# Self-attention by pairs and quads of heads, with f16 parts for Q, K, V, transposes by DMA, and a reordered last chunk before it

## The chip, the cores and the metric

The kernel runs on one core of a Trainium2 chip. The metric is the device time of one execution, in microseconds (us); less is better.

## The reference, cut to what matters

```python
# x: 1 x 256 x 512, ctx: 1 x 25088 x 512
# first attention: the 256 x 512 queries are read as 128 tokens of 16 heads of 64,
# the context as 12544 keys of 16 heads of 64
x = x + attention(layernorm(x) @ wq.T + bq, ctx @ wk.T + bk, ctx @ wv.T + bv)
# second attention
h = layernorm(x)
k, v, q = split(h @ w_in.T)                    # 512 -> 3 * 512
logits = q k^T / sqrt(32) + bias[h, i - j]     # 16 heads of 32, 256 x 256 per head
x = x + softmax(logits) @ v
x = x + mixture_of_experts(layernorm(x))       # 8 experts, top 2, hidden 1024
```

The bias is a sum of 16 Gaussians of the distance i - j, for each head.

## The kernel before

Three stages follow each other on one core; the order on each engine is the order in which the code is written, and semaphores join the engines.

**Cross-attention.** The context comes in 49 chunks of 512 rows (`NCH`), one `step(c)` each. PE projects K and V of chunk c+1 while chunk c is scored in four groups of four heads (`scores`), weighted (`weigh`) and added (`add_o`). Softmax goes through `maxima` and `p_lows` on DVE, `exps` and `p_highs` on ACT, and the running sums are rescaled on POOL. Each probability is split into two f16 parts (high on ACT, low on DVE), and both parts of a group are transposed by DMA, issued by SP (`turn_p`). f32 values are multiplied as three f16 products (`THREE`): high by high, low by high, high by low. The projected blocks share four PSUM banks (`ps_proj`), the scores have the two of `ps_s`, the output the two of `ps_o`. In the last chunk (c = 48, `NCH - 1`) no projection is left, and the scores of a group wait until the exponentials of the group before have been read from `ps_s`. SP loads all of `w_in` (3 MB) in step 47.

**Self-attention.** The residual is formed (L948), normalised, transposed on PE in f32 (`turn`), and multiplied with the f32 `w_in` (L1252, L1259). The bias rows go to DRAM and come back as diagonals (L312, L316). Then a loop over 16 heads runs one head at a time: `scores` of head h (L1272), the transposes of head h-1 on PE (L1283), the product with V of head h-3 (L1293). DVE forms logits and maxima (L987, L991), ACT the exponentials (L664), and ACT and DVE split the transposed probabilities (L657, L977).

**Experts.** 32 pieces of weights are loaded by SP (`load_piece`), split by ACT (L645) and DVE (L965), and multiplied by PE (L1316, L1339), from 1364.63 us to the end.

## Time and profile before

| | us |
|---|---|
| median of 3 runs (lowest, highest) | 1622.64 (1620.98, 1627.67) |
| the profiled execution, its own time | 1625.82 |
| its span, first to last instruction | 1624.1 |
| PE busy | 1556.1 |
| DVE busy | 1318.7 |
| ACT busy | 1260.3 |
| POOL busy | 923.4 |

The rows below are of this one execution. PE is the matrix engine, DVE the vector engine, ACT the scalar engine, POOL GpSimd; SPq is the queue of SyncE, which issues DMAs. In a timeline row the first number is the start, the second the duration in us, and in square brackets stands how long the engine sat idle before it and who released it. Times are counted from the first instruction.

### The profile page before, as it was taken

The numbers are of one execution on the slowest core, as the hardware profiler recorded it, in microseconds if no ns is written. First come the engines' busy times: TensorE is split into PE (matmuls) and PEld (weight loads), VectorE is DVE, ScalarE is ACT, GpSimd is POOL, SyncE is SP. The second block draws the span as 40 slices with busy tenths as digits, with TensorE's granted clock in tenths as the row PEclk, the third lists the DMA queues.
The fourth block names the chain that finished last, engine by engine and source line by source line (L and its number), as shares of the span: only waits on it lengthen the run. The fifth ranks groups of instructions, "written<-read, shape, count | busy, mean of one in ns | idle before, by whom it ended". The sixth has DMA issues, their size and how long they took to land.

```text
span 1624.1 us, 47795 instructions
## 1 busy us (share of the span) xinstructions
PE 1556.1 (96%) x17748; PEld 1279.1 (79%) x17748; DVE 1318.7 (81%) x1764; ACT 1260.3 (78%) x3074; POOL 923.4 (57%) x938
## 2 busy tenths in 40 slices
PE   7999999999999999999999999999997787999998
PEld 5787888888888888888888888888775555777776
DVE  7788888888888888888888888888986466767675
ACT  4888888888888888988988888888886254655554
POOL 5667678777787787787787787787752000000000
PEclk9999999999999999999999999999998766999999
DMA  4365555555555555645545545545546720555550
GB/s 175 86 135 101 136 137 115 136 131 120 136 123 123 135 119 128 140 111 134 142 107 138 138 108 136 137 115 136 129 81 157 210 103 22 201 206 194 199 206 36
DMA packets 442690, 216.03 MB, mean 133 GB/s; under 512 B 416768, under 2 KB 422912, under 8 KB 436112
## 3 DMA queue, kind: packets, MB, share of 16 engines
q1 hardware_dynamic: 442352, 215.07, 51.6%
q8 instruction: 34, 0.56, 0.1%
q10 hardware_dynamic: 288, 0.27, 0.1%
q14 instruction: 16, 0.13, 0.0%
HBM read 111.96 MB, written 0.56 MB: 69 GB/s over the span
## 4 chain that ended last, share of the span: by engine, by line
PE 85%; DVE 6%; DMA 3%; issue 2%; ACT 1%; POOL 1%; SPq 1%; DVEq 0%; POOLq 0%; ACTq 0%
PE ps_proj L1147 50%; PE ps_proj L1316 10%; PE ps_s L1193 8%; PE ps_o L1211 8%; PE ps_o L1339 5%; DMA pt_s<-p_s 2%; PE ps_proj L1176 1%; PE ps_s L1272 1%; DVE p_s L852 1%; DVE cmax L839 1%; DVE wsp L965 1%; PE ps_proj L1283 1%; POOL ctx_s L380 1%; DMA wst<-w_dram 1%; SPq L316 1%
## 5 line engine op out<-in xcount | busy, mean ns | idle before, releaser
L1147 PE MATMUL ps_proj<-wv_s,ctx_s 128*128 128x256 f16 x4032 | 482.9, 274 | 2.5 <-ACT ps_proj L529 2.5
L1147 PE MATMUL ps_proj<-ctx_s,wk_s 128*128 128x256 f16 x4032 | 480.5, 273 | 4.0 <-ACT ps_proj L527 3.1
L1147 PEld LDWEIGHTS ps_proj<-wv_s,ctx_s 128*128 128x128 f16 x4032 | 381.0, 98 | 65.4 <-issue 11.8
L1147 PEld LDWEIGHTS ps_proj<-ctx_s,wk_s 128*128 128x128 f16 x4032 | 380.0, 98 | 66.5 <-issue 24.7
L380 POOL TENSOR_TENSOR ctx_s<-t_f,ctx_s 128x512 f16<-128x512 f32 x192 | 264.0, 1384 | 279.7 <-ACT ctx_s L475 279.7
L573 ACT ACTIVATE prob<-ps_s,nmax 128x256 f32<-128x256 f32 x784 | 360.1, 475 | 14.8 <-DVE nmax L846 14.5
L839 DVE TENSOR_REDUCE cmax<-ps_s 128x4 f32<-128x1024 f32 x196 | 239.8, 1223 | 130.5 <-PE ps_s L1193 130.3
L852 DVE SCALAR_TENSOR_TENSOR p_s<-prob,p_s 128x1024 f16<-128x1024 f32 x196 | 322.0, 1643 | 2.0 <-ACT p_s L584 2.0
L380 POOL TENSOR_TENSOR ctx_s<-ctx_f,ctx_s 128x512 f16<-128x512 f32 x144 | 214.8, 1492 | 15.4 <-ACT ctx_s L470 10.7
L584 ACT ACTIVATE p_s<-prob 128x1024 f16<-128x1024 f32 x196 | 206.7, 1055 | 6.7
L1211 PE MATMUL ps_o<-v_s,pt_s 128*128 128x64 f16 x4704 | 172.2, 194 | 12.7 <-DMA pt_s<-p_s 12.7
L1316 PE MATMUL ps_proj<-x_s,wsp 128*128 128x256 f16 x1536 | 180.3, 275 | 4.2 <-issue 3.2
L1211 PEld LDWEIGHTS ps_o<-v_s,pt_s 128*128 128x128 f16 x4704 | 165.7, 99 | 22.4 <-DMA pt_s<-p_s 16.2
L1316 PEld LDWEIGHTS ps_proj<-x_s,wsp 128*128 128x128 f16 x1536 | 151.2, 99 | 36.4 <-issue 3.5
L1193 PE MATMUL ps_s<-k_s,q_s 64*128 64x256 f16 x2352 | 164.3, 273 | 6.7 <-ACT prob L573 6.6
L573 ACT ACTIVATION_READ_ACCUMULATOR prob<-ps_s,nmax 128x1 f32 x784 | 162.8, 208 | 0.0
L965 DVE SCALAR_TENSOR_TENSOR wsp<-wst,wsp 128x1024 f16<-128x1024 f32 x96 | 114.5, 1221 | 47.7 <-ACT wsp L645 47.7
L1193 PEld LDWEIGHTS ps_s<-k_s,q_s 64*128 64x128 f16 x2352 | 99.3, 94 | 58.1 <-issue 39.1
L861 DVE TENSOR_TENSOR v_s<-ps_proj,v_s 128x512 f16<-128x512 f32 x192 | 127.4, 685 | 19.2 <-ACT v_s L549 15.9
L549 ACT ACTIVATE v_s<-ps_proj 128x512 f16<-128x512 f32 x192 | 108.8, 600 | 26.1 <-PE ps_proj L1147 26.1
L645 ACT ACTIVATE wsp<-wst 128x1024 f16<-128x1024 f32 x96 | 97.4, 1049 | 19.3 <-DMA wst<-w_dram 19.2
L366 POOL TENSOR_TENSOR t_f<-ctx_f,t_f 128x512 f32<-128x512 f32 x48 | 102.7, 2140 | 0.0
(163 smaller groups left out, 1815.7 us busy)
## 6 DMA issues: line engine op xcount, KB each, us to landing
ctx_f<-ctxt_dram SPq DMA_DIRECT2D x48, 1024.0 KB, 5.8
wst<-w_dram SPq DMA_DIRECT2D x96, 512.0 KB, 4.8
pt_s<-p_s SPq DMA_TRANSPOSE x392, 2.7
w_in_sb<-w_in_dram SPq DMA_DIRECT2D x1, 3072.0 KB, 11.6
tisa<-tisa_scores SPq DMA_DIRECT2D x3, 1024.0 KB, 12.1
w_f<-wk_dram SPq DMA_DIRECT2D x2, 512.0 KB, 5.4
ctx_f<-ctxt_dram SPq DMA_DIRECT2D x2, 512.0 KB, 6.8
w_f<-wv_dram SPq DMA_DIRECT2D x1, 1024.0 KB, 9.7
```

The source lines that it names most:

```text
L380: pool.tensor_tensor(out=low[:, n, :, :], in0=sources[n], in1=high[:, n, :, :], op=ALU.subtract).then_inc(ctx_low, 1)
L549: ins = act.activation(out_v(0, odd, i, j), ps, ACT.Copy)
L573: ins = act.activation(prob[:, g % 2, (2 * b + r) * HC:(2 * b + r + 1) * HC], ps_s[:, b, r * HC:(r + 1) * HC], ACT.Exp, bias=nmax[odd][:, ...
L584: act.activation(p_s[:, g % 2, 0, :], prob[:, g % 2, :], ACT.Copy, scale=P_SCALE).then_inc(p_high, 1)
L839: dve.tensor_reduce(cmax[:, g % 2, :], ps_s[:, :, :].rearrange("p b (r k) -> p (b r) k", r=2), AX, ALU.max).then_inc(cmax_done, 1)
L852: dve.scalar_tensor_tensor(out=p_s[:, g % 2, 1, :], in0=prob[:, g % 2, :], scalar=P_SCALE, in1=p_s[:, g % 2, 0, :], op0=ALU.mult, op1=ALU. ...
L861: ins = dve.tensor_tensor(out_v(1, odd, i, j), ps, out_v(0, odd, i, j), ALU.subtract)
L965: dve.scalar_tensor_tensor(out=wsp[1][:, i % 2, n, :], in0=wst[:, i, n, :], scalar=FW_SCALE, in1=wsp[0][:, i % 2, n, :], op0=ALU.mult, op1 ...
L1147: ins = pe.matmul(ps_proj[:, bank(h, role), sub * QUARTER:(sub + 1) * QUARTER], lhsT, rhs, start=(fresh and sub == 0 and t == 0 and i == 0 ...
L1193: ins = pe.matmul(ps_s[:, head, r * HC:(r + 1) * HC], q_s[a][rows, g, r * P:(r + 1) * P], k_s[odd][b][rows, g, r * HC:(r + 1) * HC], start ...
L1211: ins = pe.matmul(ps_o[:, vg // 2, col:col + DK], pt_s[:, vg, a, 4 * head + tile, :], v_s[vodd][b][:, tile, u * DK:(u + 1) * DK], start=(i ...
L1316: ins = pe.matmul(ps_proj[:, u % 2, m * T:(m + 1) * T], wsp[a][:, (u // 2) % 2, m, col:col + P], x_s[b][:, t, :], start=(t == 0 and k == 0 ...
```

## The change

**Before self-attention.** `w_in` comes in three loads of 1 MB: K in step 46, Q and V in step 47. ACT and DVE split each into f16 parts, one instruction each for every half (`w_in_highs`, `w_in_lows`): K in step 47, Q and V after the last chunk. In the last chunk the scores of groups 1 and 3 go to `ps_proj` (`score_bank`), so two groups can be open; PE and DVE have an order of their own (`last_step`). The residual of each half is divided and added before the last product (`last_base`), which then enters in `last_o`. The bias rows leave for DRAM during the last chunk. `o_acc`, `nmax` and `lsum` are laid out by halves in all chunks, with the same instructions.

**Self-attention.** ACT and DVE split the transposed input directly from PSUM (`x_highs`, `x_lows`). Q and K of four heads come from one PSUM bank (`project_kq`: 24 products of 256 columns; `project_v2`: 12 of 512), and are split by `kq_highs`, `kq_lows`, `v2_highs` and `v2_lows`, one instruction each. Scores are made for four heads at once (`scores2`), and logits, exponentials and splits go by pairs of heads. The factor 4096 of the probabilities is a shift of the exponent, by one more small instruction. The low part is made by POOL, and the two parts are transposed by DMA (`turn_p2`) and not by PE; the pieces 1 to 3 of the experts' weights are loaded behind these transposes. The output is normalised by halves (`attended`). Lines marked "..." are left out.

```diff
-                        sp.wait_ge(ctx_low, UNITS * NCH)
-                        sp.dma_start(w_in_sb[:, :, :], w_in).then_inc(w_in_loaded, 16)
+                    for i, at, used in ((K, (NCH - 3, 0), LAST), (Q, (NCH - 2, 0), NCH), (V, (NCH - 2, 2), NCH)):
+                        if isinstance(c, int) and (c, g) == at:
+                            sp.wait_ge(ctx_low, UNITS * used)
+                            sp.dma_start(w_in_f[i][:, :, :], w_in_dram[i]).then_inc(w_in_loaded[i], 16)
+                    if isinstance(c, int) and (c, g) == (LAST, 1):
+                        sp.wait_ge(tisa_out, 1)
+                        sp.dma_start(tisa_dram.ap().rearrange("h o m -> h (o m)"),
+                                     reli[0:H2, :].bitcast(F32)).then_inc(tisa_stored, 16)
             cross_steps(sp, step)
...
+            def turn_p2(p):
+                if p >= 2:
+                    sp.wait_ge(pv2_done, 2 * (p - 1))
+                for k, split in enumerate((p2_high, p2_low)):
+                    sp.wait_ge(split, p + 1)
+                    sp.dma_start_transpose(pt2_s[:, p % 2, k, :, :], p2_s[:, p % 2, k, :]).then_inc(turned2[p % 2], 16)
+            for p in range(PAIRS):
+                turn_p2(p)
             for i in range(1, 4):
                 load_piece(i, i)
...
             cross_steps(pool, step)
+            for p in range(PAIRS):
+                half = slice(2 * (p % 2), 2 * (p % 2) + 2)
+                pool.wait_ge(p2_high, p + 1)
+                pool.tensor_tensor(out=p2_s[:, p % 2, 1, :], in0=prob2[:, half, :].rearrange("p h c -> p (h c)"),
+                                   in1=p2_s[:, p % 2, 0, :], op=ALU.subtract).then_inc(p2_low, 1)
...
+            def w_in_highs(i, half):
+                act.wait_ge(w_in_loaded[i], 16)
+                act.activation(w_in_s[i][0][:, 2 * half:2 * half + 2, :], w_in_f[i][:, 2 * half:2 * half + 2, :], ACT.Copy,
+                               scale=FW_SCALE).then_inc(w_in_high[i], 1)
...
+                    if isinstance(c, int) and c == NCH - 2:
+                        if h == 0:
+                            act.wait_ge(unit_done, units_through(2 * LAST))
+                        w_in_highs(K, h)
...
+            act.wait_ge(unit_done, units_through(2 * NCH))
+            for i in (Q, V):
+                for half in range(2):
+                    w_in_highs(i, half)
...
+            def exps2(p):
+                act.wait_ge(nmax2_done, p + 1)
+                if p >= 2:
+                    act.wait_ge(p2_low, p - 1)
+                for j in range(2):
+                    for r in range(2):
+                        slot, h = 2 * (p % 2) + j, 2 * p + j
+                        ins = act.activation(prob2[:, slot, r * T:(r + 1) * T], logit[:, slot, r * T:(r + 1) * T], ACT.Exp,
+                                             bias=nmax2[:, p % 2, 2 * j + r:2 * j + r + 1], accum_out=lsum2[:, h // 8, r, h % 8:h % 8 + 1])
+                ins.then_inc(exp2_done, 1)
+            def p2_highs(p):
+                act.wait_ge(exp2_done, p + 1)
+                if p >= 2:
+                    act.wait_ge(turned2[p % 2], 32 * (p // 2))
+                act.activation(p2_s[:, p % 2, 0, :], prob2[:, 2 * (p % 2):2 * (p % 2) + 2, :].rearrange("p h c -> p (h c)"),
+                               ACT.Copy).then_inc(p2_high, 1)
...
+            kq_highs(0)
+            kq_highs(1)
+            for p in range(PAIRS):
+                exps2(p)
+                if p < 2:
+                    kq_highs(2 + p)
+                p2_highs(p)
+                if p == 1:
+                    v2_highs(0)
+                    v2_highs(1)
...
+            def last_base(half):
+                cols = slice(NB * half, NB * half + NB)
+                dve.wait_ge(scaled, 2 * LAST + half + 1)
+                dve.wait_ge(added, 2 * LAST - 1 + half)
+                link(dve.reciprocal(l_acc[:, cols], l_acc[:, cols]))
+                acc3 = o_acc[:, half, :, :, :].rearrange("p r u d -> p (r u) d")
+                link(dve.tensor_tensor(acc3, acc3, l_acc[:, cols].unsqueeze(2).to_broadcast([P, NB, DK]), ALU.mult))
+                link(dve.scalar_tensor_tensor(out=by_rows(stream, half), in0=o_acc[:, half, :, :, :]
+                                         .rearrange("p r u d -> p r (u d)"), scalar=1.0 / (P_SCALE * W_SCALE),
+                                         in1=by_rows(xb, half), op0=ALU.mult, op1=ALU.add))
...
+            def last_o(half):
...
+                dve.wait_ge(pv_done, NG * LAST + 2 * half + 2)
+                acc3 = o_acc[:, half, :, :, :].rearrange("p r u d -> p (r u) d")
+                dve.tensor_tensor(acc3, ps_o[:, half, :].rearrange("p (u d) -> p u d", u=NB),
+                                  l_acc[:, cols].unsqueeze(2).to_broadcast([P, NB, DK]), ALU.mult).then_inc(added, 1)
+                dve.wait_ge(added, 2 * LAST + half + 1)
+                link(dve.scalar_tensor_tensor(out=by_rows(stream, half), in0=o_acc[:, half, :, :, :]
+                                              .rearrange("p r u d -> p r (u d)"), scalar=1.0 / (P_SCALE * W_SCALE),
+                                              in1=by_rows(stream, half), op0=ALU.mult, op1=ALU.add))
+                return stats(stream, half)
...
+            def last_step():
+                block_lows(LAST, 1, C21, LAST % 2)
+                maxima(LAST, 0, LAST % 2)
+                p_lows(LAST - 1, 3)
+                maxima(LAST, 1, LAST % 2)
+                add_o(LAST - 1, 0)
+                tisa_scores()
+                p_lows(LAST, 0)
+                add_o(LAST - 1, 1)
+                maxima(LAST, 2, LAST % 2)
+                p_lows(LAST, 1)
+                maxima(LAST, 3, LAST % 2)
+                last_base(0)
+                p_lows(LAST, 2)
+                p_lows(LAST, 3)
+                last_o(0)
+                last_base(1)
+                link(last_o(1))
+            cross_steps(dve, lambda c, odd: step(c, odd) if not isinstance(c, int) or c < LAST else last_step() if c == LAST else None)
...
+            w_in_lows(Q, 0)
+            w_in_lows(Q, 1)
...
+            def x_lows(i):
+                for r in range(2):
+                    dve.wait_ge(x_high, 2 * i + r - 1)
+                    dve.tensor_tensor(x_s[1][:, :, r * P:(r + 1) * P], ps_s[:, r, :].rearrange("p (t c) -> p t c", t=DT),
+                                      x_s[0][:, :, r * P:(r + 1) * P], ALU.subtract).then_inc(x_split, 1)
...
+            def logits(p):
+                if p % 2 == 0:
+                    dve.wait_ge(tisa_loaded[p // 2], 48)
+                    dve.wait_ge(s2_done, p // 2 + 1)
+                if p >= 2:
+                    dve.wait_ge(exp2_done, p - 1)
+                slots = slice(2 * (p % 2), 2 * (p % 2) + 2)
+                for j in range(2):
+                    h, slot = 2 * p + j, 2 * (p % 2) + j
+                    bias = bass.AP(tisa, h * 3 * P + 2 * P - 1, [[H2 * 3 * P, P], [P, 2], [-1, 2 * P]])
+                    ins = dve.scalar_tensor_tensor(out=logit[:, slot, :].rearrange("p (r k) -> p r k", r=2),
+                                                   in0=ps_proj[:, slot, :].rearrange("p (r k) -> p r k", r=2),
+                                                   scalar=float(HD) ** -0.5 / A_SCALE ** 2, in1=bias, op0=ALU.mult, op1=ALU.add)
+                ins.then_inc(logit_done, 1)
+                dve.wait_ge(logit_done, p + 1)
+                dve.tensor_reduce(nmax2[:, p % 2, :], logit[:, slots, :].rearrange("p h (r k) -> p (h r) k", r=2), AX, ALU.max,
+                                  negate=True).then_inc(max2_done, 1)
+                dve.wait_ge(max2_done, p + 1)
+                dve.tensor_scalar(nmax2[:, p % 2, :], nmax2[:, p % 2, :], P_SHIFT, None, ALU.add).then_inc(nmax2_done, 1)
...
+            def attended(half):
...
+                dve.wait_ge(exp2_done, 4 * half + 4)
+                link(dve.reciprocal(lsum2[:, half, :, :], lsum2[:, half, :, :]))
+                dve.wait_ge(pv2_done, 8 * half + 8)
+                link(dve.tensor_tensor(o_acc[:, half, :, :, :].rearrange("p r u d -> p (r u d)").rearrange("p (g d) -> p g d", d=HD),
+                                       ps_s[:, half, :].rearrange("p (g d) -> p g d", d=HD),
+                                       lsum2[:, half, :, :].rearrange("p r h -> p (r h)").unsqueeze(2)
+                                       .to_broadcast([P, 2 * 8, HD]), ALU.mult))
+                link(dve.scalar_tensor_tensor(out=stream[:, :, cols], in0=o_acc[:, half, :, :, :].rearrange("p r u d -> p r (u d)"),
+                                              scalar=1.0 / A_SCALE, in1=stream[:, :, cols], op0=ALU.mult, op1=ALU.add))
+                return stats(stream, half)
...
+            def last_step():
+                odd = LAST % 2
+                scores(LAST, 0, odd)
+                scores(LAST, 1, odd)
+                tisa_scores()
+                weigh(LAST - 1, 2, 1 - odd)
+                weigh(LAST - 1, 3, 1 - odd)
+                scores(LAST, 2, odd)
+                scores(LAST, 3, odd)
+                for g in range(NG):
+                    weigh(LAST, g, odd)
+            cross_steps(pe, lambda c, odd: step(c, odd) if not isinstance(c, int) or c < LAST else last_step() if c == LAST else None)
...
+            def project_kq(e):
+                if e == 0:
+                    pe.wait_ge(w_in_low[K], 2)
+                    pe.wait_ge(w_in_low[Q], 2)
+                for n, i in enumerate((K, Q)):
                     for t in range(DT):
-                        ins = pe.matmul(ps_proj[:, b + e // 2, (e % 2) * T:(e % 2 + 1) * T],
-                                        w_in_sb[:, t, base + e * P:base + (e + 1) * P], xnT[:, t, :], start=(t == 0),
-                                        stop=(t == DT - 1))
-                ins.then_inc(qkv_done, 1)
...
+            def scores2(e):
+                pe.wait_ge(kq_low, e + 1)
+                if e:
+                    pe.wait_ge(logit_done, 2 * e)
+                for r in range(2):
+                    for n, (a, b) in enumerate(THREE):
+                        for j in range(4):
+                            rows = slice(HD * j, HD * j + HD)
+                            ins = pe.matmul(ps_proj[:, j, r * T:(r + 1) * T], kq_s[a][rows, e, 1, r * P:(r + 1) * P],
+                                            kq_s[b][rows, e, 0, :], start=(n == 0), stop=(n == 2))
+                ins.then_inc(s2_done, 1)
+            def weigh2(p):
+                pe.wait_ge(turned2[p % 2], 32 * (p // 2) + 32)
...
+            project_kq(0)
+            project_kq(1)
+            scores2(0)
+            project_kq(2)
+            project_kq(3)
+            project_v2(0)
+            project_v2(1)
+            scores2(1)
+            weigh2(0)
+            scores2(2)
+            weigh2(1)
+            weigh2(2)
+            scores2(3)
+            for p in range(3, PAIRS):
+                weigh2(p)
             turn(2)
```

On PE, in the last chunk, the instructions stood in this order (`ps_s<-k_s,q_s` are the scores of a group, `ps_o<-v_s,pt_s` the weighting, the row with `tisa_e` the bias rows):

```order
L1193 MATMUL ps_s<-k_s,q_s 128x256 x12
L1211 MATMUL ps_o<-v_s,pt_s 128x64 x24
L1193 MATMUL ps_s<-k_s,q_s 128x256 x12
L1211 MATMUL ps_o<-v_s,pt_s 128x64 x24
L1108 MATMUL ps_s<-tisa_e,tsel 16x512 x2
L1211 MATMUL ps_o<-v_s,pt_s 128x64 x48
L1097 MATMUL ps_s<-ident,xn 128x128 x8
```

and now stand, from the scores of group 0 on:

```order
L1351 MATMUL ps_s<-k_s,q_s 128x256 x12
L1351 MATMUL ps_proj<-k_s,q_s 128x256 x12
L1262 MATMUL ps_proj<-tisa_e,tsel 16x512 x2
L1369 MATMUL ps_o<-v_s,pt_s 128x64 x48
L1351 MATMUL ps_s<-k_s,q_s 128x256 x12
L1351 MATMUL ps_proj<-k_s,q_s 128x256 x12
L1369 MATMUL ps_o<-v_s,pt_s 128x64 x96
L1252 MATMUL ps_s<-ident,xn 128x128 x8
```

Two groups are scored before anything is weighted, and the bias rows come third, with the weighting of the chunk before behind them. On PE, from the projections into the head loop, before:

```order
L1252 MATMUL ps_proj<-xnT,w_in_sb 128x256 x32
L1259 MATMUL ps_o<-w_in_sb,xnT 128x512 x4
L1272 MATMUL ps_s<-kT_s,qT_s 128x256 x6
L1259 MATMUL ps_o<-w_in_sb,xnT 128x512 x4
L1272 MATMUL ps_s<-kT_s,qT_s 128x256 x6
L1283 MATMUL ps_proj<-ident,prob 128x128 x4
L1272 MATMUL ps_s<-kT_s,qT_s 128x256 x6
L1283 MATMUL ps_proj<-ident,prob 128x128 x4
L1272 MATMUL ps_s<-kT_s,qT_s 128x256 x6
L1283 MATMUL ps_proj<-ident,prob 128x128 x4
L1293 MATMUL ps_proj<-v_s,pT_s 128x32 x12
L1272 MATMUL ps_s<-kT_s,qT_s 128x256 x6
```

and now, up to the last weighting (`kq_s` rows are the scores of four heads, `ps_s<-v_s,pt_s` the weighting):

```order
L1426 MATMUL ps_o<-x_s,w_in_s 128x256 x48
L1449 MATMUL ps_proj<-kq_s 128x256 x24
L1426 MATMUL ps_s<-x_s,w_in_s 128x256 x48
L1436 MATMUL ps_o<-w_in_s,x_s 128x512 x24
L1449 MATMUL ps_proj<-kq_s 128x256 x24
L1465 MATMUL ps_s<-v_s,pt_s 128x32 x24
L1449 MATMUL ps_proj<-kq_s 128x256 x24
L1465 MATMUL ps_s<-v_s,pt_s 128x32 x48
L1449 MATMUL ps_proj<-kq_s 128x256 x24
L1465 MATMUL ps_s<-v_s,pt_s 128x32 x120
```

The transposes of the probabilities are gone from PE, and there are four groups of scores in place of sixteen. On SP, from the last load of the context on, before:

```order
L272 DMA ctx_f<-ctxt_dram 128x2048
L293 DMA_TRANSPOSE pt_s<-p_s 128x8x128 x16
L307 DMA w_in_sb<-w_in_dram 128x6144
L293 DMA_TRANSPOSE pt_s<-p_s 128x8x128 x14
L312 DMA tisa_scores<-reli 16x512
L316 DMA tisa<-tisa_scores 128x16x128 x3
L323 DMA wst<-w_dram 128x1024 x3
L326 DMA wg_sb<-wg_dram 128x32
L323 DMA wst<-w_dram 128x1024 x9
```

and now, from the first load of `w_in` on (both kinds of transposes carry the name `pt_s` here; 16 of them are of self-attention):

```order
L330 DMA w_in_f<-w_in_dram 128x2048
L316 DMA_TRANSPOSE pt_s<-p_s 128x8x128 x8
L330 DMA w_in_f<-w_in_dram 128x2048
L316 DMA_TRANSPOSE pt_s<-p_s 128x8x128 x4
L330 DMA w_in_f<-w_in_dram 128x2048
L316 DMA_TRANSPOSE pt_s<-p_s 128x8x128 x6
L333 DMA tisa_scores<-reli 16x512
L316 DMA_TRANSPOSE pt_s<-p_s 128x8x128 x4
L342 DMA tisa<-tisa_scores 128x4x128 x12
L349 DMA wst<-w_dram 128x1024 x3
L352 DMA wg_sb<-wg_dram 128x32
L360 DMA_TRANSPOSE pt_s<-p_s 128x8x128 x16
L349 DMA wst<-w_dram 128x1024 x9
```

The one load of 3 MB became three with transposes between them; the bias rows moved ahead of the last four transposes of cross-attention.

## Rows read from the trace of the kernel before

**Rows 1.** The page, parts 1 and 4: busy engines, and the chain by engine

```profile
PE 1556.1 (96%) x17748; PEld 1279.1 (79%) x17748; DVE 1318.7 (81%) x1764; ACT 1260.3 (78%) x3074; POOL 923.4 (57%) x938
...
PE 85%; DVE 6%; DMA 3%; issue 2%; ACT 1%; POOL 1%; SPq 1%; DVEq 0%; POOLq 0%; ACTq 0%
```

**Rows 2.** Windows: span, busy PE PEld DVE ACT POOL (instructions), clock, DMA share, GB/s

```profile
1280.70:1303.30 22.60, 19.15 (x73) 14.79 (x74) 5.86 (x6) 6.17 (x7) 0.00 (x0) 0.93 0.96 335
1303.30:1354.10 50.80, 46.38 (x360) 31.72 (x360) 33.24 (x51) 27.35 (x82) 0.00 (x0) 0.58 0.13 50
...
1364.60:1400.00 35.40, 34.36 (x275) 26.25 (x276) 22.63 (x56) 19.84 (x31) 0.00 (x0) 0.93 0.37 134
1400.00:1621.00 221.00, 219.58 (x1672) 163.30 (x1669) 152.72 (x210) 121.32 (x193) 0.00 (x0) 1.00 0.48 171
```

**Rows 3.** Timeline, end of step 47 and last chunk (start, duration, what)

```profile
1229.04 0.57 SPq L307 DMA_DIRECT2D w_in_sb<-w_in_dram  x1
...
1233.67 1.48 PE L1147 MATMUL ps_proj<-wv_s,ctx_s 128*128 128x256 f16 x12
...
1242.62 1.13 PE L1211 MATMUL ps_o<-v_s,pt_s 128*128 128x64 f16 x24 [3.99 <-DMA pt_s<-p_s]
...
1243.57 2.75 PE L1147 MATMUL ps_proj<-wv_s,ctx_s 128*128 128x256 f16 x12
...
1246.25 0.92 PE L1193 MATMUL ps_s<-k_s,q_s 64*128 64x256 f16 x12
...
1251.31 1.46 PE L1193 MATMUL ps_s<-k_s,q_s 64*128 64x256 f16 x12 [3.34 <-ACT prob L573]
```

**Rows 4.** Timeline, from the last `p_lows` to the projections

```profile
1267.22 1.22 DVE L852 SCALAR_TENSOR_TENSOR p_s<-prob,p_s 128x1024 f16<-128x1024 f32 x1 [1.95 <-ACT p_s L584]
...
1271.40 0.87 PE L1211 MATMUL ps_o<-v_s,pt_s 128*128 128x64 f16 x24 [0.52 <-DMA pt_s<-p_s]
...
1277.93 1.97 PE L1097 MATMUL ps_s<-ident,xn 128*128 128x128 f32 x8 [5.65 <-DVE xn L725]
...
1280.68 15.71 PE L1252 MATMUL ps_proj<-xnT,w_in_sb 128*128 128x256 f32 x64 [0.78 <-DVE xnT L732]
```

**Rows 5.** Timeline, one period of the head loop

```profile
1341.33 1.46 PE L1272 MATMUL ps_s<-kT_s,qT_s 32*128 32x256 f16 x6
...
1341.52 0.51 ACT L664 ACTIVATE prob<-logit,nmax 128x256 f32<-128x256 f32 x1 [1.18 <-DVE nmax L991]
...
1342.52 0.57 ACT L657 ACTIVATE pT_s<-ps_proj 128x512 f16<-128x512 f32 x1
...
1342.83 0.69 DVE L987 SCALAR_TENSOR_TENSOR logit<-ps_s,tisa 128x512 f32<-128x512 f32 x1 [0.75 <-PE ps_s L1272]
...
1344.09 1.46 PE L1272 MATMUL ps_s<-kT_s,qT_s 32*128 32x256 f16 x6
```

**Rows 6.** Timeline, end of self-attention and start of the experts

```profile
1353.52 0.50 PE L1293 MATMUL ps_proj<-v_s,pT_s 128*128 128x32 f16 x12 [0.84 <-DVE pT_s L977]
...
1359.49 1.97 PE L1097 MATMUL ps_s<-ident,xn 128*128 128x128 f32 x8 [5.46 <-DVE xn L725]
...
1364.63 7.69 PE L1316 MATMUL ps_proj<-x_s,wsp 128*128 128x256 f16 x48 [3.17 <-issue]
```

**Rows 7.** The page, part 5: maxima, and `p_highs`

```profile
L839 DVE TENSOR_REDUCE cmax<-ps_s 128x4 f32<-128x1024 f32 x196 | 239.8, 1223 | 130.5 <-PE ps_s L1193 130.3
...
L584 ACT ACTIVATE p_s<-prob 128x1024 f16<-128x1024 f32 x196 | 206.7, 1055 | 6.7
```

**Rows 8.** Instructions of lines 380, 852 and 293, all executions

```profile
L380 POOL TENSOR_TENSOR ctx_s<-t_f,ctx_s x192: 1146/1157/2150, 31.1 to 1216.3; 128x512 f16<-128x512 f32 x192
...
L852 DVE SCALAR_TENSOR_TENSOR p_s<-prob,p_s x196: 1205/1222/2374, 56.4 to 1267.2; 128x1024 f16<-128x1024 f32 x196
...
L293 SPq DMA_TRANSPOSE pt_s<-p_s x392: 1231/1233/6652, 53.4 to 1268.6; - x196
...
DMA to landing us min/median/max: 2.7/2.7/10.3
```

More of the change, by code:

```diff
@@ L36 @@
 P_SCALE = 4096.0
+Q, K, V = range(3)
+P_SHIFT = math.log(P_SCALE)
 A_SCALE = 16.0
@@ L1290, in _ @@
+            def weigh2(p):
+                pe.wait_ge(turned2[p % 2], 32 * (p // 2) + 32)
+                if p == 0:
+                    pe.wait_ge(v2_low, 2)
+                    pe.wait_ge(kq_low, DT)
+                for j in range(2):
+                    g = 2 * p + j
                     for r in range(2):
```

307 lines of the change are left out of this document (133 added, 174 removed).

## The prediction

> **What bounds the kernel now.** I read the page first. PE is busy 96% of the span and holds 85% of the chain that ended last [rows 1], so in most of the kernel only fewer products on PE could save time. Then I read the windows over the end. From 1400 us on PE is busy 219.6 of 221 us at clock 1.00: the experts are bound by PE, and the change leaves them alone. Between 1303.3 and 1354.1 PE is busy too, but at a granted clock of 0.58, mostly its lower level (1.2 GHz), with DVE and ACT busy for 33 and 27 of 51 us [rows 2]. No other engine is full there either; what bounds that stretch is the order of the work and PE's half clock. Then I read the timeline at three seams. (1) At 1242.62 PE had waited 3.99 us for a transpose, issued behind the 3 MB load of 1229.04. Behind this wait 12 products took 2.75 us, against 1.48 before. In the last chunk PE waits 3.34 us for exponentials before it can score again [rows 3]. (2) From the last `p_lows` (ends at 1268.44) to the first transpose of the normalised residual (1277.93) pass 9.5 us, and 2.75 more to the projections [rows 4]. (3) In the head loop one head takes 2.76 us, 1344.09 less 1341.33 [rows 5], for 16 heads. The last product of the loop ends at 1354.02, the experts start at 1364.63 [rows 6], and the span ends at 1624.1: 259.5 us that I carry over unchanged.
>
> **Forecast for the last chunk.** Each of the three loads is now as large as the load of a chunk (1 MB), and the first two take the place of chunk loads that have ended. The 3.99 us wait goes, and the unit behind it runs at 1.48 instead of 2.75 us: with the shorter weighting the scores of group 0 start at 1240.7 instead of 1246.25, **-5.5**. They aren't used at once: DVE first makes the low part of half of K (1.22, the form of `p_lows` [rows 4]) and the last block, until 1243.3. Maxima (1.22 + 0.16) end at 1244.7. A group costs ACT four exponentials (1.0 for two, from 1341.52 to 1342.52 [rows 5], so 2.0) and `p_highs` 1.05 [rows 7], so groups 0 and 1 leave ACT at 1247.8 and 1250.8. Group 2 is scored behind the weighting of the old chunk's group 3, and its transposes are queued behind the load of V, issued at about 1241: I let them land at 1249.5. Weighting and scores at half clock (1.46 each [rows 3]) end at 1252.4, maxima at 1253.9, ACT frees groups 2 and 3 at 1256.9 and 1259.9, the last `p_lows` ends at 1261.1. That is 20.4 us after the first scores, before it was 22.2: **-1.8**. If V doesn't disturb, it is 3 less; if the transposes take the longest landing of the trace, 10.3 us from 1246 [rows 8], 6.8 more.
>
> From there, transposes 3.0 (1268.44 to 1271.40 [rows 4]), the weighting 1.2, and then DVE. Before, it took 5.66 from the end of the weighting (1272.27) to 1277.93. One addition of 512 columns (0.69, as L987 [rows 5]) goes, residual and statistics are for half of the columns (0.65 each saved); 3.9 remain with one more hop. PE transposes at 1269.2 instead of 1277.93, so the tail gives **-1.4**. ACT has four splits (4.2) and the table load in this time, beside the transposes. The projections must now wait for DVE: `w_in_lows` of Q (2.44), `x_lows` (2 x 0.69) and the second half of `xn`: 4.45 behind the first transpose instead of 2.75, **+1.7**. They start at 1273.65.
>
> **Forecast for self-attention.** Three f16 products replace an f32 product that costs more: 64 parts in 15.71 us [rows 4], where 96 products of 256 columns need 10.6 (12 in 1.48, tails overlapping, 2.65 for 24). But the chain no longer runs through all of them: after two of four banks PE scores four heads. The clock starts low; in the experts' first 48 products that costs 7.69 less 5.4, 2.3 us [rows 6]. So 5.3 + 2.3, the first scores 1.1, logits of a pair 2 x 0.69, maxima 1.22 [rows 7] and the shift 0.2 with hops: 11.8 us from the start, at 1285.5, ACT begins. From here ACT is the bound: 2.1 + 1.06 = 3.2 a pair, 25.6 for eight, and four splits of K, Q and V, 2.4. DVE needs 2.9 a pair. ACT still waits for DVE, since `kq_lows(2)` waits in front of the second pair's logits for a split that ACT makes only after its first exponentials (2.6), then for V's low parts (1.4), and for pairs 3, 6 and others that follow late scores (2.3): 6.3. ACT ends at 1319.8. Behind it stand POOL (2 x 1.15 = 2.3, two of its 512-column subtractions [rows 8]), the transpose 3.0, and the last weighting 1.2 with hops: 1326.7, 53 us after the projections began. Before, it was 1354.02 - 1280.68 = 73.3: **-20.3**. The transposes of PE and 16 splits from PSUM on DVE and ACT are what is saved; 2.3 + 3.0 of latency come back once.
>
> Then DVE finishes the second half only; the first half and the first piece of weights fit beside the last transposes. Product end to experts: 1.4 (division, residual), 0.7 statistics, 1.45 normalising, 2.0 transposing, 1.3 for the last split instead of copy and two splits, 0.35 hops: 7.2. Before, 1364.63 - 1354.02 = 10.6: **-3.4**. Pieces 1 to 3 are now issued at about 1325; ACT wants piece 1 some 5 us after the experts begin. I cost this at nothing; each piece later than that is a microsecond for a microsecond.
>
> Sum: -5.5 - 1.8 - 1.4 + 1.7 - 20.3 - 3.4 = -30.7, on the profiled execution's 1625.82: 1595.1. That execution is 3.2 above the median of 1622.64, so I forecast **1592**. In the other 47 chunks the changed layouts alter no instruction's size; I cost them at nothing, hidden by PE.
>
> **GpSimd beside DVE.** The trace shows mutual waits: POOL's subtraction takes 1.15 or up to 2.15 us, `p_lows` 1.21 or up to 2.37 [rows 8]. Bounds for one `p2_low`: 2.3 and 4.3. I take 2.3, since the median of all such subtractions, 1.157, lies at the low end. The Trainium skill, SBUF — State Buffer, "Who interferes with whom", says that a DVE instruction with two SBUF inputs and a GpSimd one that reads SBUF exclude each other for their whole length, and that a `tensor_reduce` never contends. By that rule only the small shift waits for POOL, and the sum stays; if the reduction waited as well, it would be some 0.5 us a pair, 4 us in all.
>
> **Rivals.**
> - *POOL sets the pace* (0.15): at 4.3 a pair against ACT's 3.2, six pairs by 1.1 and the last one by 2.0, less little that hid: +8.5, about 1600. For it speaks the doubled maximum, against it the median of 1.157 [rows 8].
> - *The heads don't overlap on PE* (0.06). Twelve products of two heads take 1.46, as six of one head do [rows 3, 5], so two heads overlap; four were never tried. One after another, 24 cost 5.1 at half clock instead of 1.5, twice on the path, and 1.5 more at first: +8.7, 1601.
> - *V's load delays the last chunk fully* (0.08): +6.8, 1599.
> - *DVE and ACT interleave better than I let them* (0.04): the 6.3 and 3 go, 1583.
> - *Transposes clog SP* (0.03), the slower side. SP issues 16 of them in a row. One issue takes 1.23 us, but up to 6.65 behind a large load [rows 8], and bias rows and piece 0 are in front of them. At 6.65 a pair would take 13.3 instead of 3.2: +81, 1673. It decides from 4.0 us an issue on: (2 x 4.0 - 3.2) x 8 = 38.
> - *Nothing comes of it* (0.02): a wait that I don't see takes the saving, 1618 to 1628.
>
> The Trainium skill, VectorE: DVE Perf Modes, "The three transpose paths", speaks against the change: a 128 x 128 transpose costs 390 ns on TensorE and 1309 ns by DMA. A pair has 16 such squares; estimated by that page alone, one after another, 20.9 us a pair, and the kernel would be over 100 us slower. The trace doesn't agree: a transpose of eight squares lands in 2.7 us here.
>
> **Numbers.** The forecast has 0.62, with its own range 1584 to 1600. The range for 8 in 10 reaches to the rivals on both sides: 1581 to 1604. A measurement of this kernel can tell about 0.5%, 8 us, from no change. Faster by more: 0.94; within: 0.03; slower by more: 0.03.
>
> **What would show it.** In the profile after: no PE wait of microseconds in step 47; two sets of scores side by side in the last chunk; its last `p_lows` near 1261; projections near 1274, and the clock up some microseconds later; ACT with exponentials and splits back to back at 3.2 a pair from 1285 on; POOL's subtraction at 2.3; experts near 1334, and 259.5 from there. The forecast is wrong if POOL's operations are above 3.2, if a transpose lands later than 3 us in self-attention, or if the experts start with a wait for a piece.

## The result, and the profile after

The changed kernel takes 1596.32 us (median of 4 runs, 1595.50 to 1597.43), the kernel before 1623.88 in the same series (4 runs, 1620.98 to 1627.67): a ratio of 0.9829, 95% interval 0.9807 to 0.9852. It is 27.6 us faster. The forecast was 1592, with 1584 to 1600 as its own range. The profiled execution took 1595.50 us, with a span of 1593.8 instead of 1624.1.

The page of the changed kernel, its parts 1 (busy time) and 4 (the chain that ended last):

```profile
PE 1512.3 (95%) x17724; PEld 1251.6 (79%) x17724; DVE 1317.6 (83%) x1767; ACT 1266.3 (79%) x3078; POOL 938.7 (59%) x946
PE 85%; DVE 6%; DMA 3%; ACT 2%; issue 2%; POOL 1%; SPq 0%; POOLq 0%; DVEq 0%; ACTq 0%
```

Beside [rows 1], PE has 43.8 us less to do and the span is 30.3 us shorter: a part of what PE no longer does has become waiting. The averages tell no more than that; the stages do. The timeline of PE in the changed kernel, from the last chunk's first scores to the projections:

```profile
1239.33 0.83 PE L1351 MATMUL ps_s<-k_s,q_s 64*128 64x256 f16 x12
1240.00 0.82 PE L1351 MATMUL ps_proj<-k_s,q_s 64*128 64x256 f16 x12
1240.75 1.89 PE L1262 MATMUL ps_proj<-tisa_e,tsel 128*16 128x512 f32 x4
1242.57 0.87 PE L1369 MATMUL ps_o<-v_s,pt_s 128*128 128x64 f16 x24
1249.73 1.46 PE L1369 MATMUL ps_o<-v_s,pt_s 128*128 128x64 f16 x24 [6.29 <-DMA pt_s<-p_s]
1251.12 1.46 PE L1351 MATMUL ps_s<-k_s,q_s 64*128 64x256 f16 x12
...
1267.35 1.46 PE L1369 MATMUL ps_o<-v_s,pt_s 128*128 128x64 f16 x24 [3.06 <-DMA pt_s<-p_s]
1272.71 1.97 PE L1252 MATMUL ps_s<-ident,xn 128*128 128x128 f32 x8 [3.90 <-DVE xn L805]
1276.64 7.09 PE L1426 MATMUL ps_o<-x_s,w_in_s 128*128 128x256 f16 x48 [1.96 <-DVE x_s L1091]
1283.66 0.83 PE L1449 MATMUL ps_proj<-kq_s 32*128 32x256 f16 x24
```

The wait of 3.99 us in step 47 [rows 3] is gone. In its place stands one of 6.29 us at 1249.73, for the transposes queued behind V's load. The scores of group 2 (1251.12) follow right behind it. I had let these transposes land at 1249.5.

Two more engines show where the waits went. DVE first, in two rows: the last low part of cross-attention, and the first instruction behind DVE's wait for the last weighting:

```profile
1260.04 1.23 DVE L943 SCALAR_TENSOR_TENSOR p_s<-prob,p_s 128x1024 f16<-128x1024 f32 x1 [0.70 <-ACT p_s L626]
...
1268.92 0.69 DVE L1009 TENSOR_TENSOR o_acc<-ps_o,l_acc 128x512 f32<-128x512 f32 x1 [3.70 <-PE ps_o L1369]
```

Then ACT in self-attention; each row is the first exponential of a pair of heads, the last one a split:

```profile
1287.78 0.51 ACT L718 ACTIVATE prob<-logit,nmax 128x256 f32<-128x256 f32 x1 [2.11 <-DVE nmax L1126]
...
1293.74 0.51 ACT L718 ACTIVATE prob<-logit,nmax 128x256 f32<-128x256 f32 x1 [2.46 <-DVE nmax L1126]
...
1299.71 0.51 ACT L718 ACTIVATE prob<-logit,nmax 128x256 f32<-128x256 f32 x1 [1.50 <-DVE nmax L1126]
...
1305.13 0.51 ACT L718 ACTIVATE prob<-logit,nmax 128x256 f32<-128x256 f32 x1 [2.26 <-DVE nmax L1126]
...
1308.20 0.49 ACT L718 ACTIVATE prob<-logit,nmax 128x256 f32<-128x256 f32 x1
...
1320.46 1.06 ACT L727 ACTIVATE p_s<-prob 128x1024 f16<-128x1024 f32 x1 [0.56 <-DMA pt_s<-p_s]
```

The first four pairs start 5.96, 5.97 and 5.42 us apart, each with a wait for DVE's maxima. From 1305.13 on ACT hardly waits, and a pair takes 3.05 to 3.55.

POOL's last subtraction, the last product of self-attention and the start of the experts, in the timelines of POOL and PE:

```profile
1321.60 2.13 POOL L495 TENSOR_TENSOR p_s<-prob,p_s 128x1024 f16<-128x1024 f32 x1 [1.45 <-ACT p_s L727]
1326.94 0.82 PE L1465 MATMUL ps_s<-v_s,pt_s 128*128 128x32 f16 x24 [1.33 <-DMA pt_s<-p_s]
1331.66 1.97 PE L1252 MATMUL ps_s<-ident,xn 128*128 128x128 f32 x8 [3.90 <-DVE xn L805]
1335.04 6.90 PE L1502 MATMUL ps_proj<-x_s,wsp 128*128 128x256 f16 x48 [1.42 <-DVE x_s L1091]
```

The windows of the changed kernel (busy time of each engine, granted clock, DMA share) are to be read beside [rows 2]:

```profile
1285.00:1303.00 18.00, 12.38 (x133) 8.39 (x134) 12.51 (x20) 11.76 (x32) 4.31 (x3) 0.93 0.31 60
1303.00:1320.00 17.00, 5.29 (x135) 3.82 (x124) 16.04 (x21) 14.16 (x44) 10.43 (x5) 0.50 0.76 128
```

In the second window DVE is busy 16.0 of 17 us and ACT 14.2, PE 5.3 at a clock of 0.50: in the head loop of before [rows 2] PE was the busiest engine, and now PE waits for the others.

### The profile page after: what moved, and what is told of

It is laid out like the page before. It is cut to its first block, busy times and chain, and to the rows that moved or that the text cites. A ratio compares the mean times of both kernels' runs of the same rounds, so it can differ in the third digit from the quotient of the medians.

```text
span 1593.8 us, 47765 instructions
## 1 busy us (share of the span) xinstructions
PE 1512.3 (95%) x17724; PEld 1251.6 (79%) x17724; DVE 1317.6 (83%) x1767; ACT 1266.3 (79%) x3078; POOL 938.7 (59%) x946
## 4 chain that ended last, share of the span: by engine, by line
PE 85%; DVE 6%; DMA 3%; ACT 2%; issue 2%; POOL 1%; SPq 0%; POOLq 0%; DVEq 0%; ACTq 0%
PE ps_proj L1301 52%; PE ps_proj L1502 10%; PE ps_s L1351 9%; PE ps_o L1369 8%; PE ps_o L1525 5%; DMA pt_s<-p_s 2%; PE ps_proj L1330 1%; DVE cmax L930 1%; DVE p_s L943 1%; POOL ctx_s L416 1%; DVE wsp L1146 1%; DMA ctx_f<-ctxt_dram 1%; ACT prob L718 0%; PE ps_o L1426 0%; ACT prob L615 0%
## 5 line engine op out<-in xcount | busy, mean ns | idle before, releaser
L615 ACT ACTIVATE prob<-ps_s,nmax 128x256 f32<-128x256 f32 x776 | 356.5, 475 | 10.5 <-DVE nmax L937 10.1
L1502 PEld LDWEIGHTS ps_proj<-x_s,wsp 128*128 128x128 f16 x1536 | 150.8, 98 | 34.3 <-DVE x_s L1091 1.8
L591 ACT ACTIVATE v_s<-ps_proj 128x512 f16<-128x512 f32 x192 | 108.8, 600 | 18.3 <-PE ps_proj L1301 18.3
L458 POOL TENSOR_TENSOR o_acc<-o_acc,alpha 128x512 f32<-128x512 f32 x98 | 103.0, 1051 | 0.0
```

Of the source, the lines that this page charges most:

```text
L591: ins = act.activation(out_v(0, odd, i, j), ps, ACT.Copy)
L615: ins = act.activation(prob[:, g % 2, (2 * b + r) * HC:(2 * b + r + 1) * HC], score_bank(c, g, b)[:, r * HC:(r + 1) * HC], ACT.Exp, bias=n ...
L1502: ins = pe.matmul(ps_proj[:, u % 2, m * T:(m + 1) * T], wsp[a][:, (u // 2) % 2, m, col:col + P], x_s[b][:, t, :], start=(t == 0 and k == 0 ...
```

## The experiments

In all experiments the transposes by DMA are plain copies of the same eight blocks of 128 x 128 through the same queue, in pieces of 256 bytes. So the weighting works on probabilities that are not transposed, and the output isn't the reference's. What is learned of the transposes by DMA themselves is therefore only what the first two kernels show.

```diff
+def blockwise(eng, dst, src):
+    return eng.dma_start(dst, src.rearrange("p (b c) -> p b c", b=8))
...
-sp.dma_start_transpose(pt_s[:, g, k, :, :], p_s[:, g % 2, k, :])
+blockwise(sp, pt_s[:, g, k, :, 0:P], p_s[:, g % 2, k, :])     # pt_s has P + 8 columns
```

### Both kernels with copies

> The kernel before with every transpose by DMA (cross-attention only) made a plain copy of the same eight blocks of 128 x 128 by the same queue, 256 bytes a piece; so the weighted values come from probabilities that are not transposed. The rest is as before. It is one half of a pair with the next run, and shows how far such a copy stands for a transpose. If a copy lands in 2 to 4 us like the transposes (2.7), the time stays within 0.5% of 1622 and the wait of 3.99 us in step 47 is there again. If copies are slower than 6 us, PE waits in every chunk and the kernel takes tens of us more.

> The changed kernel with the same replacement, in cross-attention and in self-attention. Theory A (the gain comes from fewer products on PE, work by pairs on ACT and the reordered seams; the transposes are hidden but for the last ones): the ratio to the kernel before with copies is 0.983 within 0.003, and self-attention from the first projection to the last product takes 51 us within 2. Theory B (the gain depends on what the transposes do to the queue): another ratio, by more than 0.005.

The kernel before took 1622.93 us with copies (10 runs; ratio to the original kernel before 0.998, interval 0.997 to 0.999), the changed one 1590.29 (4 runs, 0.9787, 0.9756 to 0.9818). The ratio of the two is 0.980, where with transposes it is 0.983: within the 0.003 of theory A. Self-attention takes 50.2 us, within its 51 and 2. A copy lands in a median of 3.0 us where the changed kernel's transposes need 3.1. The seams look the same: in the kernel before with copies PE waits 4.95 us in step 47, in the changed one 6.19 us behind V's load. So a copy can stand for a transpose almost everywhere. The table shows where it can't; all times are differences between events of one profile.

| stretch, us | before | before, copies | after | after, copies |
|---|---|---|---|---|
| start to scores of group 0, last chunk | 1246.25 | 1242.85 | 1239.33 | 1237.59 |
| to the end of the last `p_lows` | 22.2 | 22.4 | 21.9 | 21.8 |
| to the transposes of the residual | 9.5 | 9.5 | 11.4 | 9.2 |
| to the projections | 2.8 | 2.8 | 3.9 | 3.9 |
| to the end of the last product | 73.3 | 73.5 | 51.1 | 50.2 |
| to the experts | 10.6 | 10.6 | 7.3 | 7.3 |
| to the end of the span | 259.5 | 259.5 | 258.8 | 258.8 |

The third row is the exception. In the changed kernel the last weighting of cross-attention starts 6.1 us after the last low part, with copies 3.8.

The first row moves without a cause in the code. The changed kernel with copies and the five experiments below make a family of six, and five of these are the same up to the scores of group 0, which start at 1235.5 to 1237.6 us. Stretches repeat better. The second row is 21.5 to 21.9 us in the four of the family that leave the last chunk alone. In self-attention the first 48 projections vary from 6.8 to 8.1 us, but from the first scores to the last product the four that leave self-attention alone take 43.53, 43.53, 43.55 and 43.56. So the experiments are read by such stretches and not by dates, each in one execution.

### The bias rows later

```diff
+            sp.wait_ge(pv_done, CROSS_PV)
             for e in range(DT):
                 ...                       # the 12 loads of the bias rows
-            sp.wait_ge(pv_done, CROSS_PV)
```

> The changed kernel with copies for transposes, and the 12 loads of the bias rows issued by SP only when PE has weighted the last group of cross-attention. Theory A (these loads, issued beside the last group's transfers, make them land 6.1 us after the last low part instead of 3.0 in the changed kernel): the time from the last low part to the last weighting shrinks by up to 3 us, as far as the copies are late at all beside the loads, the loads end in front of the first logits and are hidden, and the kernel gains as much. Theory B (they are late by themselves, two issued close behind the group before): this time stays within 0.7 us and the kernel too.

1590.84 us (4 runs; 0.979, 0.9766 to 0.9814), against 1590.29 without the edit. The queue of SP shows that the edit did what it says: the 12 loads begin at 1264.50 and no longer at 1260.16, where they came right behind the last copies.

```profile
1255.13 4.75 SPq L77 DMA_DIRECT2D pt_s<-p_s  x4
1264.50 9.90 SPq L347 DMA_DIRECT2D tisa<-tisa_scores  x12
```

From the last low part to the last weighting it still took 3.8 us: theory B. For copies, then, the loads behind them cost nothing. For transposes no run has the edit: the last one took 6.1 us beside the loads in the changed kernel and 3.0 without them in the one before.

The two traces say more. From the issue of the last transpose to its landing, first the changed kernel (1262.21 to 1267.30), then the one before (1268.62 to 1271.35); the rows give a queue's packets, and the landing of the transpose:

```profile
q8 instruction: 1, 0.02, 1.1%
pt_s<-p_s SPq DMA_TRANSPOSE x1, 5.1
...
q1 hardware_dynamic: 1998, 0.50, 80.8%
pt_s<-p_s SPq DMA_TRANSPOSE x1, 2.7
```

In the changed kernel one packet of 16 KB of the kernel's own instructions went through the DMA engines in this time (1265.23, 0.92 us); in the kernel before there was none. The last packet of 256 bytes, the size of the transposes' pieces, had started at 1265.22, 3.0 us after the issue, so what came late was the end of the transfer and not its data. I sorted all 408 transposes of the changed kernel by what was in flight beside them. With neither a load nor such an instruction packet 234 landed in 3.0 to 3.4 us, median 3.06. With loads issued only behind them, 49 landed in 3.0 to 3.3, median 3.05. With a load ahead of them, 89 had a median of 4.75. With an instruction packet alone, 23 landed in 3.0 to 5.0, median 3.9. Loads behind a transpose cost it nothing in 49 cases, although those moved pieces larger than the bias rows' 512 bytes; the instruction packet is the likelier cause. It explains the lateness by where it stood, and no run moved it.

### V's load later

```diff
-(V, (NCH - 2, 2), NCH)
+(V, (NCH - 2, 3), NCH)
```

> The changed kernel with copies for transposes, and the load of V's weights issued behind the transfers of group 3 of chunk 47, not in front of them. Theory A (V's 1 MB makes PE wait, 6.29 us in the changed kernel, and the scores of group 2 stand behind that wait): the weighting comes up to 3 us earlier, the scores of groups 2 and 3 too, and the last low part of cross-attention comes 2 to 3 us earlier after the scores of group 0. Rival B: ACT's four sets of exponentials and splits are already back to back, so that PE's wait is not on the path: within 0.7 us. Rival C: the transfers of group 0 of the last chunk are late in its place, which shows as a wait ahead of that weighting but costs nothing.

1589.37 us (4 runs; 0.9786, 0.9765 to 0.9807). The difference to 1590.29 is too small for the runs, but the profile shows it. PE's timeline with V's load behind the copies of group 3:

```profile
1237.66 0.83 PE L1355 MATMUL ps_s<-k_s,q_s 64*128 64x256 f16 x12
...
1245.84 1.46 PE L1373 MATMUL ps_o<-v_s,pt_s 128*128 128x64 f16 x24 [4.07 <-DMA pt_s<-p_s]
1247.23 1.46 PE L1355 MATMUL ps_s<-k_s,q_s 64*128 64x256 f16 x12
...
1252.11 1.36 PE L1373 MATMUL ps_o<-v_s,pt_s 128*128 128x64 f16 x24 [2.62 <-DMA pt_s<-p_s]
```

The wait shrinks from 6.19 to 4.07, and from the scores of group 0 to the last low part it takes 19.7 us instead of 21.8. Theory A holds: 2.1 us. Rival C's wait is there too (2.62 at 1252.11, for the transfers now behind V). Neither ACT nor DVE waits for it, so it costs nothing here. The 4.07 that remain aren't V's: DVE makes this group's low part from 1241.44 to 1242.66, behind the maxima of the last chunk's group 0, and the weighting starts 3.2 us later.

### One place for the last chunk's scores

```diff
-return ps_proj[:, head, :] if isinstance(c, int) and c == LAST and g % 2 else ps_s[:, head, :]
+return ps_s[:, head, :]
...
-                if isinstance(c, int) and c == LAST and g == 1:
-                    pe.wait_ge(block_low, 8 * LAST + 7)
-                elif isinstance(c, int) and c == LAST and g >= 2:
-                    pe.wait_ge(exp_done, NG * c + g - 1)
-                elif g >= 1 or after(c, -1):
+                if g >= 1 or after(c, -1):
                     pe.wait_ge(exp_done, NG * c + g)
...
                 scores(LAST, 0, odd)
-                scores(LAST, 1, odd)
+                pe.wait_ge(block_low, 8 * LAST + 7)
                 tisa_scores()
                 weigh(LAST - 1, 2, 1 - odd)
+                scores(LAST, 1, odd)
```

> The changed kernel with copies for transposes, and the last chunk's scores all in the one place of the other chunks: PE scores groups 1 to 3 each only when the exponentials of the group before are read. Theory A (the second place is worth what my forecast gave it, 1.8 us, and up to 3 more where V's transfers are not the limit): the time from the scores of group 0 to the last low part grows by 1.8 to 5 us. Rival B (the late transfers of group 3 of chunk 47 set the end of this stretch in either arrangement): within 0.7 us, and then the second place has brought nothing here.

1592.90 us (4 runs; 0.9812, 0.979 to 0.9835). PE now waits for exponentials before groups 1 and 3, 2.44 and 3.49 us:

```profile
1241.59 0.83 PE L1351 MATMUL ps_s<-k_s,q_s 64*128 64x256 f16 x12 [2.44 <-ACT prob L619]
1245.44 1.46 PE L1369 MATMUL ps_o<-v_s,pt_s 128*128 128x64 f16 x24 [3.03 <-DMA pt_s<-p_s]
1246.84 1.46 PE L1351 MATMUL ps_s<-k_s,q_s 64*128 64x256 f16 x12
1251.79 1.46 PE L1351 MATMUL ps_s<-k_s,q_s 64*128 64x256 f16 x12 [3.49 <-ACT prob L619]
```

The stretch takes 23.3 us instead of 21.8. So the second place is worth 1.5 us, a little less than theory A's lower end. Group 2 is scored at nearly the same distance from group 0 as with two places (11.1 against 11.7 us), because it waits for V's load in both; what the second place saves lies in group 3.

### The low parts of K and Q behind the second pair

```diff
                 logits(p)
-                if p < 2:
-                    kq_lows(2 + p)
+                if p == 1:
+                    kq_lows(2)
+                    kq_lows(3)
```

> The changed kernel with copies for transposes (as in the run before this one, which it is compared with), and one more change: the low parts of the third and fourth bank of K and Q are made behind the logits of pair 1 on DVE, and no longer in front of the logits of pairs 1 and 2. Theory A (my forecast's 6.3 us of waits are the order of DVE's work): ACT's wait of some 2.5 us ahead of the second pair's exponentials goes, pairs 0 and 1 follow each other at 3.6 to 3.8 us, the second set of four heads can be scored about 2.7 us earlier, and the time from the first projection to the last product shrinks by 2.5 to 5 us. Theory B (the first pairs are bound by something behind the split, the second set's scores or V's low parts): the wait only moves to pair 2, and the stretch stays within 1 us.

1589.87 us (4 runs; 0.9795, 0.9771 to 0.9818). The stretch from the first projection to the last product went from 50.2 to 49.2 us, and counted from the first scores from 43.5, which repeats within 0.03, to 42.5. ACT's rows, the first exponentials of pairs 0 and 2:

```profile
1280.96 0.51 ACT L722 ACTIVATE prob<-logit,nmax 128x256 f32<-128x256 f32 x1 [2.11 <-DVE nmax L1130]
1291.86 0.51 ACT L722 ACTIVATE prob<-logit,nmax 128x256 f32<-128x256 f32 x1 [3.02 <-DVE nmax L1130]
```

Pair 1 has no row with a wait any more, it starts 3.4 us behind pair 0 (5.97 without the edit). But pair 2 now waits 3.02 us, where it waited 1.50. DVE and PE at that point:

```profile
1289.08 1.29 DVE L1122 SCALAR_TENSOR_TENSOR logit<-ps_proj,tisa 128x512 f32<-128x512 f32 x2 [1.45 <-PE ps_proj L1454]
1282.86 5.34 PE L1441 MATMUL ps_o<-w_in_s,x_s 128*128 128x512 f16 x24
1288.14 0.83 PE L1454 MATMUL ps_proj<-kq_s 32*128 32x256 f16 x24
```

DVE waits for the scores of pair 2, and these stand on PE behind V's products (5.34 us). Theory A is right for pair 1 and theory B for the sum: 1.0 us is gained of 2.5. The scores of the second four heads in front of V's products would be the next edit; it wasn't tried.

### Transposes on PE, and one set of scores head by head

```diff
+pe.transpose(ps_o[:, j, q * P:(q + 1) * P], prob2[:, 2 * (p % 2) + j, q * P:(q + 1) * P], ident[:, :])
+act.activation(pt2_s[:, p % 2, 0, :, 0:P], ps_o ..., ACT.Copy)
+dve.tensor_tensor(pt2_s[:, p % 2, 1, :, 0:P], ps_o ..., pt2_s[:, p % 2, 0, :, 0:P], ALU.subtract)
...
+n, j = (i % 3, i // 3) if e == 0 else (i // 4, i % 4)      # product i of 12, part n, head j
```

> The changed kernel with plain copies for the transposes of cross-attention (so their result isn't transposed), and in self-attention two more edits. (1) The probabilities are transposed on PE in f32 (8 squares a pair into PSUM) and split from there by ACT (high part, a pair behind the exponentials) and by DVE (low part); POOL has nothing to do in self-attention; projections, scores of four heads and work by pairs stay. (2) The first set of scores alone (24 products at full clock, so far 0.83 us) is written head by head. For (1): theory A (the transposes by DMA are worth what they take off DVE): DVE becomes the bound at 2.9 + 1.2 = 4.1 us a pair instead of ACT's 3.2, V must be split before pair 0 is turned, and the last transfer of 3.0 and POOL's 2.1 at the end go: first projection to last product takes 53 to 60 us instead of 50.2. Theory B (half clock and the chain through PE set the pace, as in the kernel before with its 73.3): 60 to 70. Theory C (the transposes by DMA bring nothing, the gain is all projections and pairs): 51 or less. For (2): theory A (four heads overlap only when they stand side by side): 2.5 to 2.6 us; theory B (the order doesn't matter): 0.83. And since POOL rests, DVE's shift of 128 x 4 should take 0.17 every time, where it took up to 1.75, and the residual's addition 0.7 instead of 2.66, if it was POOL that they waited for.

1600.39 us (4 runs; 0.9847, 0.9828 to 0.9865), 10.1 more than with copies. The first projection to the last product takes 57.3 us instead of 50.2, and the end to the experts 10.0 instead of 7.3, since DVE's last low part and the first piece of weights now stand in front of the second half's residual. One pair in the second half of the loop, rows of PE, ACT and DVE:

```profile
1315.68 1.94 PE L1485 MATMUL ps_o<-ident,prob 128*128 128x128 f32 x8 [2.08 <-DVE pt_s L1157]
1317.65 1.02 ACT L724 ACTIVATE pt_s<-ps_o 128x1024 f16<-128x1024 f32 x1 [1.14 <-PE ps_o L1485]
1318.71 1.22 DVE L1157 TENSOR_TENSOR pt_s<-ps_o,pt_s 128x1024 f16<-128x1024 f32 x1 [0.53 <-ACT pt_s L724]
1320.08 1.94 PE L1485 MATMUL ps_o<-ident,prob 128*128 128x128 f32 x8 [1.82 <-DVE pt_s L1157]
```

A pair takes 4.4 us here (1320.08 less 1315.68): 1.94 on PE, 1.02 on ACT, 1.22 on DVE, one after the other, since there is one place in PSUM for the transposed pair. A second place wasn't tried. In the middle of the loop, exponentials to exponentials, it is 3.9 to 4.4, with DVE busy 18.3 of the 20 us from 1300. So the size of theory A came out (53 to 60), but the late pairs are bound by this chain and not by DVE alone. Of the 7.1 us, 1.4 come from the first 48 projections (8.12 against 6.76 us), which the edit doesn't touch and which had a mean granted clock of 0.65 here and 0.79 there.

The scores head by head, in PE's and DVE's timeline:

```profile
1280.36 0.85 PE L1459 MATMUL ps_proj<-kq_s 32*128 32x256 f16 x24
1281.14 5.41 PE L1436 MATMUL ps_s<-x_s,w_in_s 128*128 128x256 f16 x48
1281.70 1.28 DVE L1118 SCALAR_TENSOR_TENSOR logit<-ps_proj,tisa 128x512 f32<-128x512 f32 x2
```

0.85 us against 0.83, and PE's next products start 0.78 us behind the first of the scores: theory B. A matmul's end in these rows is modelled. But DVE used the scores 1.34 us after PE began on them, without a wait, so 2.5 us are out in any case. For these 24 products the order of the heads doesn't matter.

With POOL at rest all eight shifts of DVE took 0.17 us, and the residual's addition 0.69. In the changed kernel they took up to 1.75 and 2.66:

```profile
1303.35 1.75 DVE L1126 TENSOR_SCALAR nmax<-nmax 128x4 f32<-128x4 f32 x1
1318.03 2.66 DVE L1138 SCALAR_TENSOR_TENSOR stream<-o_acc,stream 128x512 f32<-128x512 f32 x1
```

At both times POOL was subtracting (1302.95 to 1305.07 and 1318.02 to 1320.14). The Trainium skill, SBUF — State Buffer, "Who interferes with whom", names both kinds among those that can contend with GpSimd, a `tensor_scalar` and an instruction with two SBUF inputs, and exempts the reduction; the traces agree, the reductions took 1.22 with and without POOL.

## Why the prediction was right, and where it wasn't

The forecast was 1592 us, and the median is 1596.3: 4.3 more, inside the range. By the profiled executions it was 30.7 us off, and 30.3 came off; by the medians 27.6, since the profiled execution of before lay above its median and that of after below. That 30.3 meets 30.7 is partly luck. The steps were off by -1.4, +1.5, +3.3, -0.5, -1.9, +0.1 and -0.7 us, and these cancel. The largest term, self-attention, and its mechanism came out; one step failed.

- **Step 47, -5.5: measured -6.9.** The mechanism was right (no wait, the unit at full clock); scores began 1.4 us earlier than I had put them. Most of that isn't the step's. From the first scores of chunk 47 to those of chunk 48 it took 23.29 us instead of 28.97, which is -5.7; the other 1.2 us were there when step 47 began, and no step of the sum had them.
- **Last chunk, -1.8: measured -0.3.** The last low part ended at 1261.27, predicted 1261.1. V's load was issued at 1239.91, 1.1 us earlier than I had put it, but the transposes behind it landed at 1249.7, only 0.2 off: they took 9.8 us from that issue and not 8.5. So the 1.4 us of the first step were waited away there. With copies V's load costs 2.1 us, shown by moving it; the second place brings 1.5, shown by taking it away. I had said 3 for V.
- **Tail, -1.4: measured +1.9. This step failed.** "Transposes 3.0" was taken from the kernel before, where SP had nothing else in its queue. In the changed kernel it was 6.1. The rest of the step (1.2 and 3.9) came to 5.4. The rows show two parts. SP began the last issue 0.9 us after the low part (1262.2 against 1261.27), because it was still issuing the high part's transpose, 1.24 us from 1260.86; before, it began 0.2 us after. And the transpose landed 5.1 us after its issue instead of 2.7. That the bias rows queued behind it are the cause would have been my guess; with copies they aren't, and 49 other transposes with loads behind them weren't late. A packet of instructions beside it fits, as shown above, but wasn't tried, so the cause of these 2.4 us stays open.
- **To the projections, +1.7: measured +1.2.** DVE's order is as described, without the hop that I had added.
- **Self-attention, -20.3: measured -22.2.** First exponentials after 11.1 us (11.8 predicted), ACT's part 33.7 (34.3), POOL 2.1 (2.3), the last transpose 3.1 (3.0). The sum of ACT's waits, 6.3, was 7.3: 2.46 + 1.50 + 2.26 for DVE and 1.1 for transposes. The causes that I named for them were half right: without the low part in front of pair 1's logits its wait goes, but V's products on PE stand behind it.
- **Product to experts, -3.4: measured -3.3.** Experts +0: measured -0.7, no step had it.
- "What is saved" in self-attention: transposes on PE instead of transfers, with one place in PSUM, cost 10.1 us of the 32.6 between the two kernels with copies (and of the 10.1, 1.4 are the clock of the first projections and 2.7 my order behind the loop). So two thirds of the gain or more are left for the f16 products, the work by pairs and the seams. No run took one of these away from self-attention alone, so that share is a remainder and not a measurement.

Of the rivals, *POOL sets the pace* fell: each subtraction took 2.12 or 2.13, and POOL rested 0.92 to 1.45 us between the late ones. *The heads don't overlap* fell: 24 products in 0.83 us, in either order. *V's load delays fully* fell: the transposes behind it landed at 1249.7, not at 1256.3. *DVE and ACT interleave better* fell: ACT waited 7.3 us. *Transposes clog SP* fell: SP issued the 16 in 33.7 us and they landed in 3.1 (median; 4.8 at most). *Nothing comes of it* fell: 27.6 us came.

Of the forecast's own signs of being wrong two stayed away: POOL took 2.1 and the experts waited for no piece. The third, a transpose later than 3 us in self-attention, came, and it was drawn too tight. Thirteen of the 16 landed in 3.0 to 3.3 us. The other three took 4.1, 4.6 and 4.8, and they are the three with a 16 KB instruction packet in flight (1303.72 and 1322.16). None of the three was on the path, since the last product waited for the transpose behind them.

The Trainium skill, VectorE: DVE Perf Modes, "The three transpose paths", was weighed in the forecast as speaking against the change. The last experiment agrees with it on which engine is faster, not by how much: PE turns eight squares of f32 in 1.94 us, mostly at its lower clock (0.54 granted from 1315 to 1320), and the DMA needs 3.1 for eight of f16, and two sets of them a pair. But the kernel with PE's transposes is the slower one. Their result lies in PSUM, DVE has to make the low part from there (1.22 us a pair), and PE, ACT and DVE wait for each other, while the DMA works beside them.

Moving V's load and the low parts brought 2.1 and 1.0 us apart. Together that is 0.2% and below what this measurement can tell from nothing; the two weren't run together.

## What to carry to other kernels

A latency that is taken from a quiet place in the old order is not that of the new one: look at what the changed kernel puts in the same queue just ahead, and give it a range. Here a load ahead of a transpose made 3.06 us into 4.75 (medians), and a load behind it changed nothing. A wait behind a load shrinks when the load is issued later, here by 2.1 us. Compare stretches between two events, since dates drift between executions of the same code. And check whether a sum that comes out did so term by term. When an edit takes a wait away, find the next condition of the same instruction on every engine: behind DVE's order stood PE's.
